# Second feed-forward pass: the first two of three inner tiles taken through gelu, cast and split by one operation each

## The reference

```python
def _quantize_activations_groupwise(x):      # five groups along the batch
    gamma = jnp.max(jnp.abs(ag))
    xq = clip(ag * QB / (gamma + EPS), -QB + EPS, QB - EPS)

def _bitlinear(x, W, b):
    Wb = _binarize_weights_groupwise(W)      # signs
    y = jnp.einsum('btc,oc->bto', x, Wb) + b
    return _quantize_activations_groupwise(y)

h = _bitlinear(h_in, W1, b1)                 # 96 -> 384
h = jax.nn.gelu(h, approximate=False)
out = _bitlinear(h, W2, b2)                  # 384 -> 96
```

## Time and profile before

| | |
|---|---|
| time, median of 3 runs | 874.72 us (872.73 to 875.58) |
| the profiled execution | 873.6 us, of which the span of the profile is 871.8 us |
| PE busy in the span | 804.3 us (92%) |
| DVE busy | 645.0 us (74%) |
| ACT busy | 448.5 us (51%) |
| POOL busy | 190.3 us (22%) |
| DVE low part, L1494 | 60 operations, 56.8 us busy, 17.1 us idle ahead of them |
| ACT gelu, L775 | 90 operations, 80.5 us busy, 12.7 us idle ahead of them |
| ACT cast, L784 | 60 operations, 51.5 us busy |

### The profile page before, as it was taken

How to read it: one execution, slowest core, us unless ns; L and a number is a source line. 1 busy time by engine, 2 the same in 40 slices (tenths; PEclk the granted TensorE clock), 3 DMA queues, 4 the chain that set the end, 5 groups by cost and what they waited for, 6 DMA issues and landing times.

```text
span 871.8 us, 17975 instructions
## 1 busy us (share of the span) xinstructions
PE 804.3 (92%) x6053; PEld 622.4 (71%) x6053; DVE 645.0 (74%) x1998; ACT 448.5 (51%) x619; POOL 190.3 (22%) x218
## 2 busy tenths in 40 slices
PE   1889799999999999999999999999999799979991
PEld 0556478888888888888888888888888655545540
DVE  4875367877777777777777777777777367978987
ACT  0132335455454454454454454454453499968981
POOL 2750022323223323223223223222222000000000
PEclk9999889999999999999999999999999899989996
DMA  9930001100001000001000011000010001463434
GB/s 213 230 85 1 15 15 46 40 29 28 28 28 53 30 28 28 28 28 55 28 28 28 28 29 54 28 28 28 28 42 14 28 28 49 132 161 99 128 111 124
DMA packets 19886, 48.54 MB, mean 56 GB/s; under 512 B 4558, under 2 KB 4754, under 8 KB 19858
## 3 DMA queue, kind: packets, MB, share of 16 engines
q1 hardware_dynamic: 17024, 46.97, 19.5%
q10 hardware_dynamic: 2834, 1.21, 0.8%
HBM read 29.51 MB, written 18.67 MB: 55 GB/s over the span
## 4 chain that ended last, share of the span: by engine, by line
PE 76%; DVE 6%; issue 5%; DMA 4%; ACT 4%; POOL 3%; ACTq 2%; DVEq 0%; SPq 0%; POOLq 0%
PE slot L962 17%; PE slot L943 12%; PE slot L822 10%; PE slot L1008 9%; PE slot L1129 5%; PE slot L969 5%; PE slot L972 5%; PE slot L1100 4%; PE slot L957 3%; DMA xs<-out 2%; PE slot L1161 2%; DMA out<-xs 2%; ACTq L602 2%; PE slot L1165 1%; ACT hT L775 1%
## 5 line engine op out<-in xcount | busy, mean ns | idle before, releaser
L962 PE MATMUL slot<-w2s,hT 128*112 128x96 f32 x1344 | 162.7, 269 | 0.0
L1377 DVE TENSOR_SCALAR xh<-t,ln_mv,ln_rs 112x96 f32<-112x96 f32 x434 | 109.2, 323 | 60.1 <-POOL ln_rs L579 60.1
L962 PEld LDWEIGHTS slot<-w2s,hT 128*112 128x112 f32 x1344 | 141.6, 177 | 10.8
L712 ACT ACTIVATE hT<-slot,b1c,w_unit 128x784 f32<-128x784 f32 x96 | 95.9, 1005 | 95.6 <-PE slot L943 95.6
L719 ACT ACTIVATE stage<-slot,minus_one 112x768 f32<-112x768 f32 x64 | 52.6, 821 | 117.9 <-PE slot L1008 117.9
L552 POOL TENSOR_TENSOR xn_lo<-xn,xn_hi 96x784 f16<-96x784 f32 x32 | 53.4, 1670 | 247.5 <-ACT xn_hi L701 247.3
L579 POOL TENSOR_TENSOR ln_rs<-ln_ve,pow_half 112x7 f32<-112x7 f32 x62 | 92.0, 1483 | 4.9
L969 PE MATMUL slot<-big,W1b 99*128 (+1 forms) x360 | 89.4, 329 | 0.6 <-ACT hT L775 0.6
L972 PE MATMUL slot<-big,W1b 96*128 (+1 forms) x360 | 89.2, 328 | 0.0
L1383 DVE TENSOR_REDUCE ymax<-slot 128x784 f32 (+1 forms) x90 | 83.8, 960 | 6.2 <-PE slot L972 5.9
L775 ACT ACTIVATE hT<-slot,s 128x784 f32<-128x784 f32 x90 | 80.5, 929 | 12.7 <-DVE stage L1494 12.6
(11 more groups left out here) (189 smaller groups left out, 1364.6 us busy)
## 6 DMA issues: line engine op xcount, KB each, us to landing
xs<-in_x SPq DMA_DIRECT2D x32, 294.0 KB, 3.1
out<-t2T SPq DMA_DIRECT2D x32, 294.0 KB, 3.3
big<-in_x SPq DMA_DIRECT2D x7, 1176.0 KB, 11.8
xs<-out SPq DMA_DIRECT2D x24, 294.0 KB, 3.2
out<-xs SPq DMA_DIRECT2D x24, 294.0 KB, 2.6
big<-out SPq DMA_DIRECT2D x1, 1764.0 KB, 11.4
out<-big SPq DMA_DIRECT2D x6, 294.0 KB, 2.6
big<-in_x SPq DMA_DIRECT2D x2, 588.0 KB, 5.7
```

The source lines that it names most:

```text
L712: nc.scalar.activation(hT[:, t, :].rearrange("p (a n) -> p a n", a=2), halves((0, one, 2)[t], P), ACT.Relu, scale=w1_unit[:, t:t + 1], bia ...
L962: ins = mm(o[:, j, :], hT[:, t, j * TOK:(j + 1) * TOK], w2s[:, v, t, :], start=False, stop=t == TILES - 1, skip_group_check=True)
L1377: ins = V.tensor_scalar(dst[:, j, :], src[:, j, :], ln_mv[n][:, j, 0:1], ln_rs[n][:, j:j + 1], ALU.subtract, ALU.mult)
```

## The change

The four PSUM slots become one tensor of eight banks, so that one operation can read two slots. Tiles 0 and 1 of an image go through gelu as one operation of 1568 columns over slots 0 and 1, through the cast as one, and through the low part as one; tile 2 stays alone. ACT's order becomes gelu 0 and 1, cast 0 and 1, gelu 2, `y2_out(b - 1)`. The counters `gelu_ready` and `parts_ready` rise by two per image instead of three, `hi_parts` by one instead of two. The gelu of image 0's first tile is no longer issued ahead of L735. The products on PE, their order and the transfers are the same.

```diff
@@ -136,7 +136,8 @@
         ctx.enter_context(nc.allow_low_precision(reason="float32 carried as exact parts"))
 
 
-        S = [ctx.enter_context(nc.psum_tensor(f"slot{k}", [P, 2, 512], F32)) for k in range(4)]
+        slots = ctx.enter_context(nc.psum_tensor("slots", [P, 8, 512], F32))
+        S = [slots[:, 2 * k:2 * k + 2, :] for k in range(4)]
 
         def one_other(r):
             return (1, 3) if r == 0 else (3, 1)
@@ -769,42 +770,38 @@
 
 
 
-            def gelu_tile(g, b, t):
-                wait_count(act, parts_ready, 3 * b + t - 2)
-                wait_apart(act, y1_ready, 3 * b + t + 1, act_passed)
-                nc.scalar.activation(gel[:, t, :].rearrange("p (a n) -> p a n", a=2), halves(t, P),
+            def gelu_tiles(g, b, t, n, done):
+                wait_count(act, parts_ready, 2 * b - 2 + done)
+                wait_apart(act, y1_ready, 3 * b + t + n, act_passed)
+                nc.scalar.activation(gel[:, t:t + n, :].rearrange("p t (a n) -> p (t a) n", a=2),
+                                     slots[:, 2 * t:2 * (t + n), 0:HALF],
                                      ACT.Gelu, scale=s1[:, bass.ds(g, 1)]).then_inc(gelu_ready, 1)
 
-            def gelu_hi(b, t, r):
-                wait_apart(act, gelu_ready, 3 * b + t + 1, act_passed)
-                if t == 0:
-                    wait_count(act, y2_ready, b - 1)
-                    if not isinstance(b, int):
-                        act.sem_inc(act_passed, 1)
-                nc.scalar.copy(h_hi[r][:, t, :], gel[:, t, :]).then_inc(hi_parts, 1)
+            def gelu_hi(b, r):
+                wait_apart(act, gelu_ready, 2 * b + 1, act_passed)
+                wait_count(act, y2_ready, b - 1)
+                if not isinstance(b, int):
+                    act.sem_inc(act_passed, 1)
+                nc.scalar.copy(h_hi[r][:, :, :], gel[:, 0:SPLIT, :]).then_inc(hi_parts, 1)
 
             def y2_out(b):
                 wait_apart(act, y2_ready, b + 1, act_passed)
                 nc.scalar.activation(y2_all[:, b, :].rearrange("p (a n) -> p a n", a=2), halves(3, C),
                                      ACT.Identity, bias=fb2c[:, 0:1]).then_inc(y2_evac, 1)
 
-            def ffn(g, m, started=False):
+            def ffn(g, m):
                 for r in range(2):
                     b = 2 * m + r
-                    if not (started and r == 0):
-                        gelu_tile(g, b, 0)
-                    gelu_tile(g, b, 1)
-                    gelu_hi(b, 0, r)
-                    gelu_tile(g, b, 2)
-                    gelu_hi(b, 1, r)
+                    gelu_tiles(g, b, 0, SPLIT, 1)
+                    gelu_hi(b, r)
+                    gelu_tiles(g, b, SPLIT, 1, 2)
                     if not (isinstance(b, int) and b == 0):
                         y2_out(b - 1)
 
             nc.scalar.activation(gelu_warm[:, :], minus_one[:, :], ACT.Gelu)
             act.wait_ge(s1_ready, 1)
-            gelu_tile(0, 0, 0)
             step(LAST // 2, 1, experts=False, attend=False, ffn=False)
-            ffn(0, 0, started=True)
+            ffn(0, 0)
             with act.Fori(1, QB // 2) as q:
                 ffn(0, q)
             with act.Fori(1, QGROUPS) as g:
@@ -1142,7 +1139,7 @@
 
             def ffn_up(b, scale=None, t0=0):
                 for t in range(t0, TILES):
-                    wait_count(pe, gelu_ready, 3 * b + t - 2)
+                    wait_count(pe, gelu_ready, 2 * b - 1 + (t == TILES - 1))
                     ffn_tile(b, t, t).then_inc(y1_ready, 1)
                     if scale is not None and t == 1:
                         wait_count(pe, y2_evac, b - 1)
@@ -1154,13 +1151,13 @@
                 if isinstance(b, int) and b == 0:
                     pe.wait_ge(t2T_evac, BATCH)
                 wait_count(pe, y2_evac, b)
+                pe.wait_ge(parts_ready, 2 * b + 1)
                 for t in range(SPLIT):
-                    pe.wait_ge(parts_ready, 3 * b + t + 1)
                     for part, src in enumerate((h_hi[r], h_lo[r])):
                         for h in range(2):
                             mm(S[3][0:C, h, 0:HALF], W2b[:, t, :], src[:, t, h * HALF:(h + 1) * HALF],
                                start=t == 0 and part == 0, stop=False, skip_group_check=True)
-                pe.wait_ge(parts_ready, 3 * b + TILES)
+                pe.wait_ge(parts_ready, 2 * b + 2)
                 for h in range(2):
                     ins = mm(S[3][0:C, h, 0:HALF], W2last[:, :], h_last[r][:, h * HALF:(h + 1) * HALF],
                              start=False, stop=True, skip_group_check=True)
@@ -1489,11 +1486,10 @@
 
             def split(m, r):
                 b = 2 * m + r
-                for t in range(SPLIT):
-                    dve.wait_ge(hi_parts, SPLIT * b + t + 1)
-                    V.scalar_tensor_tensor(h_lo[r][:, t, :], gel[:, t, :], Q_CLIP, h_hi[r][:, t, :],
-                                           ALU.min, ALU.subtract).then_inc(parts_ready, 1)
-                dve.wait_ge(gelu_ready, 3 * b + 3)
+                dve.wait_ge(hi_parts, b + 1)
+                V.scalar_tensor_tensor(h_lo[r][:, :, :], gel[:, 0:SPLIT, :], Q_CLIP, h_hi[r][:, :, :],
+                                       ALU.min, ALU.subtract).then_inc(parts_ready, 1)
+                dve.wait_ge(gelu_ready, 2 * b + 2)
                 V.tensor_scalar(h_last[r][:, :], gel[:, 2, :], Q_CLIP, None, ALU.min).then_inc(parts_ready, 1)
 
             def y2_absmax(b):
```

## The result

The change makes the kernel slower: 884.84 us (884.29 to 887.45, 4 runs) against 873.73 us (871.72 to 875.58, 4 runs), a ratio of 1.013 with a 95% interval of 1.011 to 1.015. The forecast was 884.8. The profiled execution took 887.45 us, the highest of the four, with a span of 885.0.

A forecast was written before the change was run, and what follows sets the result against it. Merging was predicted to make one `gel` copy's gelu-cast-low-part ring the bound, 5.27 us an image instead of 4.7. With late places the end comes 10.1 us later: 883.7 profiled, 884.8 us median, range 880.5 to 891.

The forecast's parts named there:

- What bounds the kernel: Second pass before the change: ACT, PE and DVE each have about 4.7 us per image; the `gel` waits, 4.44, don't bind.
- Durations: Merged operations, from slopes per column: gelu 1.58 us, cast 1.51, low part 1.79, chosen between 1.75 and 1.85.
- The ring: Single `gel`: merged gelu, cast, low part and handovers must end before the next image's gelu; 5.27 us a turn.
- ACT's own work: ACT's work per image in the second pass falls from 4.68 to about 4.45 us through merging.
- the signs that I had named: Groups 0 to 4: gelus 5.2 to 5.35 us apart, ACT idle 0.6 to 0.8 ahead of each, ended by low part.
- the rival of a faster kernel: Beat follows ACT's work, 4.68 to 4.45 us, 29 times 0.23 = 6.7 us saved: 868 us; chance 0.04.
- Group starts: Second image of groups 1 to 4: DVE's longer list delays the gelu, 12.67 us for two turns instead of 10.54.
- The transfer: Load for the last group keeps its 19.87 us span; low part of image 15 2.23 us late, gelu 16 at 784.97.
- The sum: First-gelu starts through the second pass: image 29's at 857.74 instead of 847.67, so the end comes 10.1 us later.
- the late places swallow the ring: Rival: waits at four group starts (2.1 us) and the transfer (2.2) are spare time for longer turns: 874 us; chance 0.07.
- merging saves nothing: Rival: merged operations take what two take, new handover 0.25, 5.67 us a turn, 8 us more: 893 us; chance 0.04.
- the clock falls: Rival: PE's idling lowers its clock at group starts too, each costing 1.5 to 3 us: 891 to 895 us; chance 0.05.

The follow-up runs named there:

- The first experiment: The change with a second copy of `gel`, everything still merged, each image using its own copy: 879.13 us, ratio 1.0053 to the kernel before.
- the one with gelu 2 in the ring: The change with one copy of `gel` and gelu 2 moved ahead of the merged cast: 897.58 us, ratio 1.028.

## Why the prediction was right

**What bounds the kernel.** Right. Before, three engines with 4.7 us of work and a ring of 4.44 beneath them. The second copy of `gel` in the kernel before left its turns at 4.68.

**Durations.** Merged gelu 1.57 us (1.58 foretold), cast 1.50 (1.51), low part 1.79 (1.79). The slopes of the earlier trace rows carried over from other operations of the same engines, and the choice between 1.75 and 1.85 was good. It was a choice, and no row decided it.

**The ring.** 5.36 us, foretold 5.27. Handing over from cast to low part took 0.03, from DVE to ACT 0.21 and 0.29. The one that was off is the new one, from the gelu to its own cast: 0.19 and 0.25 by turns (734.60 and 729.31 less the ends of their gelus), where the earlier trace rows gave 0.11. I had named 0.25 as its other end. Over 20 turns that is nearly 2 us. In images 0 and 1, whose waits have constant counts, it was 0.12 and 0.11, as foretold; only in the loops it is longer:

```profile
694.05 1.56 ACT L776 ACTIVATE hT<-slots,s 128x1568 f32<-128x1568 f32 x1
695.73 1.50 ACT L785 CAST stage<-hT 128x1568 f16<-128x1568 f32 x1
```

**ACT's own work.** Wrong, with no effect on the sum: I had it fall to 4.45. Its list is 4.80, since that handover is part of it, more than before. The first experiment showed it. It also shows in the signs that I had named: ACT's idle time ahead of a merged gelu is 0.42 and 0.50 us, not 0.6 to 0.8. And the rival of a faster kernel was worked out from that 4.45; at a pace set by a list of 4.80 the change would have been slower too.

**The places out of beat.** Group starts: 12.67 us over two turns was foretold, 5.36 + 7.31 = 12.67 measured, and 12.35 at the first one; the turn behind it takes 5.46 to 5.52, for a wait for the `xs` load that I had put at nothing. The transfer: a turn of 7.50 foretold, 7.15 measured, and then one of 5.73, in which PE still ran at 1.2 GHz after its idle time. PE stayed off the ring by 1.4 us, where over 1 was said, and DVE behind the ring had 0.74 and 0.50 us idle, where 0.67 was said.

**The sum.** Starts of merged gelus in the profile: image 0 at 694.05 (694.16), 9 at 745.19 (743.72), 15 at 779.45 (777.47), 16 at 786.60 (784.97). Image 29's came at 860.75 against 857.74. Of these 3.0 us the ring makes 1.8 and image 2 makes 1.6, and the rest cancels. Image 2's gelu waited for PE, which had idled 1.08 and 0.92 us for ACT's gelus and then ran at a granted clock of 0.51:

```profile
697.70:704.60 6.90, 6.50 (x17) 3.31 (x18) 4.02 (x4) 4.22 (x4) 0.00 (x0) 0.51 0.29 87
```

```profile
695.67 0.51 PE L966 MATMUL slots<-big,W1b 99*128 99x392 f16 x2 [1.08 <-ACT hT L776]
...
698.10 0.83 PE L966 MATMUL slots<-big,W1b 99*128 99x392 f16 x2 [0.92 <-ACT hT L776]
...
699.38 2.82 PE L1158 MATMUL slots<-stage,W2b 128*96 128x392 f16 x8
701.99 2.69 PE L1162 MATMUL slots<-stage,W2last 128*96 128x392 f32 x4
```

The eight and four matmuls of this `ffn_down` took 5.1 us, 2.7 at the full clock. The prediction had the first images cost nothing: it looked for a fall of the clock at group starts and at the transfer, not here. It may well belong to merging the gelus. The profiles of four experiments with merged gelus ahead of their casts (two copies, low part split, gelu alone with one copy and with two) show PE idle 1.08 and then 0.92 to 1.01 us at the same two places, and at 1.2 GHz from the second of them on, for 3.4 to 6.8 us. The kernel before, the one with only the low part merged and the one with gelu 2 in the ring stayed at 1.00 from 696 to 706. The remaining three profiles came to the pass at 1.2 GHz already and say nothing on this. The other three executions of the change have no trace, so it isn't known how long it was there.

The profiled execution was foretold at 883.7 us and took 887.45, 3.75 more: the 3.0 up to image 29's gelu, 0.1 behind it, and 0.65 outside the span. The median lies 2.6 us lower. So the median's agreement to the decimal is luck: the difference of the medians is 884.84 - 873.73 = 11.1 us, foretold 10.1, and the median of before has itself moved by 1.

**The rivals.** ACT's work as the pace fell with the first turn. That the late places swallow the ring: beyond what was in the sum they swallowed 0.35 us at the transfer and 0.32 at the first group start. The turn behind the transfer gave back the 0.37 us by which it was longer. That merging saves nothing: it saved 0.14 us on the gelus, 0.09 on the casts and 0.06 on the low parts, and it did not matter. That the clock falls: it did once more than before, for 6.8 us at the pass's start, and it accounts for 1.6 us there. The two merges tried alone, of gelus and of low parts, both lost, and the low parts' lost more than everything together. The cast alone wasn't tried. The Trainium skill, Perfetto Trace Analysis, section Optimizing Scalar/DVE Operations, has it that where these engines aren't saturated but hold up others, breaking instructions up may let work finish sooner. The runs with one copy agree with it where the kernel before is the one broken up (903.50, 884.84 and 880.29 us against 873.73 to 874.34). They don't where only the low part is: with gelu and cast merged, two low parts gave 889.75 us and turns of 5.41 to 5.43, one gave 884.84 and 5.36, since the merged gelu waits for both anyway.

## What to carry to other kernels

Before merging operations on tiles, draw the ring from the buffer's first writer to its last reader and back, with whole durations and a handover at every change of engine: with one copy of the buffer the merged ring is the sum of the merged operations, and the split one hides each behind the other. Merging one member alone can be worse than merging all, as the low part showed. A merge also makes the next operation on the same engine wait for the whole result; where it stands directly behind, that wait (0.22 us here) ate the fixed part that was saved. If the merge is wanted, give the buffer a second copy first and then look for the next ring, which goes through the engine that consumes the result.

## What the runs showed of the hardware that was not expected

A dependent operation on ACT directly behind the one it needs started at three distances from the recorded end. In images 0 and 1, where the counts of the waits are constants, the cast started 0.12 and 0.11 us behind its gelu, as in the first pass. In a loop's body the counts are in registers: in the second image of the body, where the list has one register instruction between gelu and cast, it was 0.19, and in the first, where the program has two (one ahead of each of the cast's two waits), 0.25 to 0.26. So each register instruction goes with 0.07 us more. That is read from the lists and the trace; no run took one out.

At the changeover between the passes the granted clock of TensorE differs from profile to profile, and up to the pass's first gelu the code is the same. Windows of two profiles there, of the change and of the kernel with two copies and gelu 2 ahead of the cast (stretch, length, busy us of PE, PEld, DVE, ACT, POOL, PEclk, DMA share, GB/s):

```profile
678.00:694.00 16.00, 13.18 (x82) 11.63 (x83) 4.30 (x10) 5.87 (x9) 0.00 (x0) 0.81 0.07 20
694.00:704.00 10.00, 8.00 (x28) 3.96 (x27) 3.86 (x3) 7.81 (x7) 0.00 (x0) 0.68 0.30 90
```

```profile
678.00:694.00 16.00, 12.23 (x62) 10.49 (x62) 7.03 (x18) 3.49 (x5) 0.92 (x1) 0.65 0.07 20
694.00:704.00 10.00, 8.16 (x34) 5.79 (x32) 0.85 (x1) 4.11 (x6) 0.00 (x0) 0.54 0.10 30
```

```profile
681.43 0.88 PE L821 MATMUL slots<-con,xh 112*96 112x112 f32 x7 [2.37 <-DVE xh L1376]
```

The granted clock is 1.00 at 2.4 GHz and 0.50 at 1.2. By these rows PE ran at 1.2 GHz for 2 x 0.19 x 16 = 6.1 us and 2 x 0.32 x 10 = 6.4 us in the change, and for 2 x 0.35 x 16 + 2 x 0.46 x 10 = 20.4 us in the other, whose first merged gelu started at 702.42 instead of 694.05. In both PE had been idle for 2.37 us at that place, up to 677.85 in the change and up to the row at 681.43 in the other. The clock fell at 677.1 in the change, during that idle time, and was back at 1.00 at 683.9; in the other it fell at 682.7, behind it, and was back only at 703.2. The kernel before has 0.81 in the first window too, and 1.00 in the second; the second window is in the changed code, and what it has to do with the merged gelu is told above. No run was made to steer the clock. Differences of 2 to 3 us between such kernels are better read from the turns than from one execution's time.
